# A graph network kernel on one core: x loaded in six parts, one pair of tiles computed whole, two DMA issues set apart

## What is computed

```python
h = relu(layernorm(x))
x = x + (adj.T @ h) * inv_deg[:, None]        # inv_deg = 1 / adj.sum(axis=0), inf -> 0
h = relu(layernorm(x))
x1 = silu((adj @ h) @ W + b)
x2 = silu((adj @ x1) @ W + b)
return x + x2
```

## Time and profile before

| | |
|---|---|
| median of three runs | 626.46 us |
| profiled execution: time | 627.91 us |
| its span | 626.1 us |
| PE, DVE, POOL, ACT busy | 97%, 87%, 87%, 55% |
| granted TensorE clock | 0.998 (the 2.4 GHz level) |
| HBM rate over the span | 315 GB/s |
| DMA queues from 300 to 400 us, share of 16 engines | SP's 54.9%, ScalarE's 55.1% |

### The profile page before, as it was taken

How to read it: one execution, slowest core, us unless ns; L and a number is a source line. 1 busy time by engine, 2 the same in 40 slices (tenths; PEclk the granted TensorE clock), 3 DMA queues, 4 the chain that set the end, 5 groups by cost and what they waited for, 6 DMA issues and landing times.

```text
span 626.1 us, 6939 instructions
## 1 busy us (share of the span) xinstructions
PE 609.1 (97%) x2296; PEld 413.3 (66%) x2296; DVE 541.8 (87%) x558; ACT 345.8 (55%) x456; POOL 544.2 (87%) x281
## 2 busy tenths in 40 slices
PE   8888999999999999999999999999999999999996
PEld 5355666577565567667667667777677677677774
DVE  5899699787868999897998998997998998998991
ACT  2493686595263354756656646646555546456551
POOL 2499799599688588999999989997999999998991
PEclk9999999999999999999999999999999999999999
DMA  9998999889999899999999999909999999999961
GB/s 324 382 372 301 339 320 358 293 329 275 353 351 367 287 345 334 347 347 347 347 347 348 347 348 347 283 25 220 308 348 349 348 349 348 348 348 349 348 176 34
DMA packets 151492, 197.73 MB, mean 316 GB/s; under 512 B 5280, under 2 KB 134560, under 8 KB 151456
## 3 DMA queue, kind: packets, MB, share of 16 engines
q1 hardware_dynamic: 86176, 132.92, 63.9%
q10 hardware_dynamic: 65280, 64.36, 33.6%
HBM read 195.17 MB, written 2.10 MB: 315 GB/s over the span
## 4 chain that ended last, share of the span: by engine, by line
PE 63%; POOL 10%; DMA 9%; issue 6%; DVE 6%; ACT 3%; ACTq 2%; SPq 1%; POOLq 0%; DVEq 0%
PE dg L444 14%; PE dg L461 11%; PE dg L451 11%; PE dg L450 11%; DMA raw<-in_adj_dram 9%; PE m_ps L367 7%; POOL a_lo L855 5%; POOL at_lo L203 3%; PE m_ps L372 2%; PE m_ps L387 2%; PE m_ps L373 2%; DVE dg L699 2%; PE m_ps L474 2%; ACTq L285 2%; DVE turned L744 2%
## 5 line engine op out<-in xcount | busy, mean ns | idle before, releaser
L203 POOL TENSOR_TENSOR at_lo<-turned,at_hi 128x1024 fp32r<-128x1024 f32 x152 | 358.9, 2402 | 26.5 <-ACT at_hi L584 26.4
L744 DVE STREAM_TRANSPOSE turned<-raw 128x1024 f32<-128x1024 f32 x216 | 257.7, 1221 | 20.2 <-PE dg L461 13.9
L584 ACT ACTIVATE at_hi<-turned 128x1024 fp32r<-128x1024 f32 x152 | 157.0, 1055 | 97.8 <-DVE turned L744 71.1
L855 POOL TENSOR_TENSOR a_lo<-raw,a_hi 128x1024 fp32r<-128x1024 f32 x62 | 145.9, 2391 | 21.7 <-ACT a_hi L542 21.6
L699 DVE TENSOR_TENSOR dg<-raw,dg 128x2048 f32<-128x2048 f32 x60 | 137.5, 2291 | 29.2 <-DMA raw<-in_adj_dram 27.6
L450 PE MATMUL dg<-at_hi,f_hi 128*128 128x512 f32 x384 | 152.4, 397 | 0.3 <-ACT at_hi L584 0.2
L451 PE MATMUL dg<-at_hi,f_lo 128*128 128x512 f32 x384 | 151.3, 394 | 0.0
L461 PE MATMUL dg<-at_lo,f_hi 128*128 128x512 f32 x384 | 145.1, 459 | 1.2 <-POOL at_lo L203 1.2
L444 PE MATMUL dg<-turned,f_w 128*128 128x512 f32 x256 | 120.2, 592 | 0.0
L367 PE MATMUL m_ps<-raw,h 128*128 128x512 f32 x264 | 117.8, 593 | 2.5 <-DMA raw<-in_adj_dram 1.7
L461 PEld LDWEIGHTS dg<-at_lo,f_hi 128*128 128x128 f32 x384 | 72.1, 188 | 43.3 <-issue 28.9
(11 more groups left out here) (55 smaller groups left out, 338.1 us busy)
## 6 DMA issues: line engine op xcount, KB each, us to landing
raw<-in_adj_dram SPq DMA_DIRECT2D x64, 1024.0 KB, 7.3
raw<-in_adj_dram ACTq DMA_DIRECT2D x122, 512.0 KB, 14.2
raw<-in_adj_dram SPq DMA_DIRECT2D x118, 512.0 KB, 12.5
out_dram<-x SPq DMA_DIRECT2D x12, 128.0 KB, 6.6
x_rows<-in_x_dram SPq DMA_DIRECT2D x2, 256.0 KB, 5.4
x_rows<-in_x_dram SPq DMA_DIRECT2D x1, 512.0 KB, 11.2
out_dram<-x SPq DMA_DIRECT2D x4, 64.0 KB, 1.8
out_dram<-x ACTq DMA_DIRECT2D x4, 64.0 KB, 2.0
```

The lines of the kernel that those rows point to most:

```text
L203: return eng.tensor_tensor(at_lo[:, place(unit)], turned_tile(unit), at_hi[:, ring3(s)].bitcast(f32), ALU.subtract)
L584: act.activation(at_hi[:, ring3(s)], turned_tile(unit), ACT.Copy).then_inc(hi3_done, 1)
L744: dve.transpose(dst, src).then_inc(t3_done, 1)
L855: pool.tensor_tensor(a_lo[:, s % RING1], raw1[:, v % RAW1, i], a_hi[:, s % RING1].bitcast(f32), ALU.subtract).then_inc(lo1_done, 1)
```

## The change

x is loaded in six parts: tiles 0 to 1 and 2 to 3 ahead of pair 0, 4 to 7 ahead of pair 1, 8 to 15 ahead of pair 3, 16 to 23 ahead of pair 5 and 24 to 31 ahead of pair 7. VectorE takes the statistics of the first two parts at the start and those of each other part behind the degree sum of the pair ahead of the one that it was issued with. POOL does the scale and shift of the first five parts at the start and that of the sixth after `lo1` of pair 6.

Pair 8 is whole in quarter 0, and its row becomes a late one. As `copy_nodes` and the norm steps go by split pairs, quarter 0 has five of these instead of six.

In sweeps 2 and 3 ScalarE issues block 2 of a piece where it issued both, and block 3 two units later.

```diff
-HEAD = ((0, 4), (4, 8), (8, 16), (16, 32))
-HEAD_PAIRS = (0, 2, 3, 4)
+HEAD = ((0, 2), (2, 4), (4, 8), (8, 16), (16, 24), (24, 32))
+HEAD_PAIRS = (0, 0, 1, 3, 5, 7)
-WHOLE1_FIRST = (0, 1, 2, 3, 4, 5, 7, 10, 13, 15)
-LATE_ROWS = (2, 3, 5)
-SPLIT_ROWS = (6, 8, 9, 11, 12, 14) + LATE_ROWS
+WHOLE1_FIRST = (0, 1, 2, 3, 4, 5, 7, 8, 10, 13, 15)
+LATE_ROWS = (2, 3, 5, 8)
+SPLIT_ROWS = (6, 9, 11, 12, 14) + LATE_ROWS
+        def head_parts(v):
+            return [b for b in range(len(HEAD)) if HEAD_PAIRS[b] == v]
@@ SP, ahead of load1(v)
-                if v in HEAD_PAIRS:
-                    b = HEAD_PAIRS.index(v)
+                for b in head_parts(v):
@@ ScalarE, units of sweeps 2 and 3
-                if unit == 1:
-                    load3(act, 3, ACT_BLOCKS)
-                if unit % QU == 0 and RAW3 <= i < len(PIECES) and i not in KEPT:
-                    load3(act, i, ACT_BLOCKS)
+                if unit in (1, 3):
+                    load3(act, 3, ACT_BLOCKS[unit // 2:unit // 2 + 1])
+                if unit % QU in (0, 2) and RAW3 <= i < len(PIECES) and i not in KEPT:
+                    load3(act, i, ACT_BLOCKS[unit % QU // 2:unit % QU // 2 + 1])
@@ VectorE
-            head(0)
+            for b in head_parts(0):
+                head(b)
             for v in range(QUARTERS * PAIRS):
                 add_degrees(v)
-                if v < len(HEAD) - 1:
-                    head(v + 1)
+                for b in head_parts(v + 1):
+                    head(b)
@@ POOL
-            for b, (lo, hi) in enumerate(HEAD):
+            for b, (lo, hi) in enumerate(HEAD[:-1]):
                 scale_shift(lo, hi, b)
@@ POOL, after lo1(v)
+                if v == splits1[0]:
+                    scale_shift(*HEAD[-1], len(HEAD) - 1)
```

## The result

The changed kernel takes 623.15 us (621.82 to 625.75, nine runs) against 626.46 (625.06 to 627.19), a ratio of 0.9955 (0.9941 to 0.9969). By the medians that is 3.3 us less, by the ratio 2.8, with 1.9 to 3.7 as its interval. A second comparison gave 0.9958 (0.9944 to 0.9972). The forecast was 622.7. The profiled execution was the longest of the nine: 625.75 us, span 624.0, which is 2.6 us over the median; that of the kernel before was 1.45 us over its own. A difference between two profiles therefore holds some of the spread between executions.

A forecast was written before the change was run, and what follows sets the result against it. POOL was taken to bound pairs 6 to 12, PE the rest from the quarter's end. Head 2.75 plus issues 1.0 made 3.75 us off the 626.1 span (622.35), or 622.7 from the median; range 620.9 to 626.3.

The forecast's parts named there:

- Quarter 0: First quarter of sweep 1: smaller x loads and whole pair 8 start pair 12 at 48.95 instead of 51.70, gaining 2.75 us.
- The chain: Quarter 0's sequence of loads, POOL and PE: pair 9's load at 37.0, its lo from 38.0, pair 12 at 48.95.
- I let the whole 2.75 us through: Quarters 1 to 3: later loads move along with PE and POOL, so the whole 2.75 us lasts to the end.
- the sixteenth copy: Copy of x moving behind pair 44: first block of piece 0 some 3.7 us later, turned after 206, costing nothing.
- quarter 3's air: PE's gaps in quarter 3, 2.6 us over a sum of 53.2, at loads released as in the other quarters.
- The fourth copy: Copy of x before the first message addition: VectorE waits about 1.5 us; cost nothing, without cover up to 1.5 us.
- The two issues: ScalarE's block issues in sweep 2, set two units apart: POOL regains 1.57 us, partly met by loads; 1.0 us taken.
- my upper bound of 2.0: Most that separating the issues could gain: PE's open and half-hidden waits in sweep 2 before 301, 2.0 us.
- the first (head alone): Rival, chance 0.22: the issues' stall only moves and POOL stays late; only the head gains 2.75 us, giving 623.7.
- The second: Rival, chance 0.20: the last part's late norm holds POOL before pair 9, pair 12 at 50.7; gain 1.0, 625.5 us.
- The third: Rival, chance 0.13: ScalarE's second block lands 0.5 us late on some 11 pieces in the later sweeps; slower, 629.2 us.

The follow-up runs named there:

- the second run: The changed kernel with the copies of x begun one split pair earlier (COPY_FROM 5 instead of 6), run once more on another chip: 621.62 us, 0.9917 of the kernel before.

## Why the prediction was right, and where it was not

The median was 0.45 us from the forecast, and that is partly luck. In the profiles the span shrank by 2.1 us and not by 3.75: 0.8 us too much was forecast for quarter 0, 2.1 us of loss in quarter 3 were not seen, and 1.3 us too little was taken for the issues. These errors cancel only in part. The medians lie 3.3 us apart, and the ratio's 2.8 us (1.9 to 3.7) stop just short of the 3.75 forecast.

- **Quarter 0**: 1.95 us in the first profile for 2.75. The chain was the right one; pair 9's load landed at 37.70 instead of the 37.0 that I carried over from the earlier trace rows, and everything behind it (lo at 38.83 for 38.0, pair 12 at 49.75 for 48.95) moved with it. That landing varies by 1 us (36.81 to 37.76) between the profiles with pair 8 whole. The profile thus can't tell a wrong sum from an ordinary late load.
- **Who earns it**: the prediction summed the six parts and pair 8 in one chain and never asked for each alone. In its own working pair 9 waits for its load from 36.0 to 37.0: that was the sign that POOL's earlier start is worth nothing. The runs show all of quarter 0's gain with pair 8 alone, and a loss of 1.95 us with the parts alone.
- **"I let the whole 2.75 us through"**: right for quarters 1 and 2, wrong for quarter 3, and the step that failed is the next one, the sixteenth copy: "it is turned after 206, so again nothing". I asked who waits for the moved block and not what it meets in its queue. In the queue it meets the second block and the loads of pairs 47 to 50, with the DMA share at 1.02 to 1.06: pair 50 landed at 172.85, where with the copies earlier (the second run) it landed at 169.25. Between the two kernels with x in four parts that differ in this, its price was 2.0 us. Between the two with x in six it was 1.0 us, which their intervals do not tell from nothing. Nor was quarter 3's air 2.6 us: the sum gave 53.2 us for a quarter without gaps, and the shortest took 52.82.
- **The fourth copy**: VectorE waited 1.17 us where I said 1.5, and nothing came of it, as said. The profile after has it as

```profile
86.70 1.12 DVE L730 SCALAR_TENSOR_TENSOR x<-tp,inv_deg,x 128x128 f32<-128x128 f32 x4 [1.17 <-ACT x L529]
```

- **The two issues**: the mechanism was right and mis-sized, 2.3 us for 1.0, and over my upper bound of 2.0. That bound was PE's air in the stretch up to 301, and this is where the gain was made. I took half of it for fear of the loads, and VectorE's waits for them rose only from 3.6 to 4.2 us, with its short ones ahead of `dg` from 4.0 to 5.2. PE's open waits for at_lo give 0.9 us of the 2.3 (1.2 to 0.3); its weight loads' waits for at_lo, which partly hide behind matmuls, fell from 2.5 to 0.7. ScalarE's sequencer spends 39 us on issues of blocks from 224 to 330 instead of 59.
- **Rivals**: the first (head alone) had the shares reversed, since it is the issues that stay whole. The second named a mechanism that didn't occur, since the last part's norm was done at 36.2 us and pair 9's load came later. The third, a late second block, didn't happen: ScalarE's blocks land in 14.3 us from 230 to 300, against 15.3 in the earlier trace rows, and from 300 to 400 in 14.4 against 14.2. By the Trainium skill (DMA: Bandwidth & Descriptors, Issuing engines are not separate DMA queues) issuing is usually small against the transfer. The trace disagrees for this stretch: one issue took up to 2.5 us and two together 5.01 beside a landing time of 14.3 to 15.3, and setting them apart was worth 2.3 us.

What stays open is why quarter 3 is long. It took 55.9 and 57.0 us in two profiles with the blocks 8.9 us apart (the kernel before, issues only), and 52.8 to 53.4 in four with them 7.8 to 8.0 apart. In all six the first block goes out 17.5 us ahead of quarter 2's end, so neither its place in the quarter nor the distance alone explains it. In the two long ones this first block had already taken 10.2 and 10.3 us to land, in the four 5.3 to 9.2, and the second goes out after the rounding of pair 46, which waits for that pair's load: part of the distance is a result of slow loads and not their cause. The profiles are single executions. Nor was it tried why the rate falls beside a block to 32 partitions.

## What to carry to other kernels

Cost each edit of a bundle alone in the chain, and stop at the first wait that another resource sets: an engine that starts earlier ahead of a load that doesn't come earlier wins nothing. Compare kernels that ran beside each other, and repeat a small difference: one kernel here measured 0.9950 and 0.9917. For a transfer that moves, look not only at who waits for it but at what is in the queue where it lands. And where the engines behind it wait for an engine that computes and also issues DMAs, as in the first 80 us of sweep 2, its issues belong apart from each other, beside its waits; later in the sweeps the same edit won nothing.

## What the runs showed of the hardware

A DMA share over 100% does not tell the rate: with a share of 1.02 and 1.04 the same queues moved 362 and 334 GB/s over 54 us, in two kernels that differ in when the first of four 512 KB blocks with 1 KB rows to 32 partitions was sent. In single 4 us slices of one kernel it was 213 GB/s at a share of 1.08 with two such blocks in flight and 410 at 1.03 with none.

Nor does the share tell what an issue costs the engine that makes it. In the changed kernel ScalarE's issues of the four blocks of piece 0 took 0.32 to 0.39 us each, with the share at 0.96 to 1.08 around them. From 230 to 300, at 1.10, one took up to 2.5 us. There 23 blocks of 14.3 us each were sent in 70 us, by estimate 4.7 of them in flight at a time, against two at most of those of piece 0. Which of the two, the share or the blocks in flight, makes an issue long was not tried.
